# New piece orders for all engines of a two-layer transformer kernel, and one added wait

## What is computed

```python
x = x + L0_attn(layernorm(x))   # 16 heads of 16, window 64, plus a memory branch
#   q, k = rope(rms_norm(q)), rope(rms_norm(k))
#   attn_out = softmax(masked q k^T) v @ w_o
#   q_mem = (softmax(masked q k^T) * decay * gamma) k
#   phi = silu(q_mem @ mem_w1); mem_out = (phi + phi**2) @ mem_w2
#   x1 = x + attn_out * sigmoid(mem_out)
#   x1 + (silu(y @ ffn_w1) * (y @ ffn_w3)) @ ffn_w2,  y = rms_norm(x1)
x = x + L0_ffn(layernorm(x))    # relu(x @ up) @ down + sum(softmax(top2)) * (x @ expert)
x = x + L1_attn(layernorm(x))   # latent attention, 16 heads of 128, no mask
x = x + L1_ffn(layernorm(x))    # 16 experts of 176, top 6 of a softmax, plus a shared expert of 352
```

## Time and profile before

| | |
|---|---|
| median of 3 runs | 762.76 us (762.37 to 765.84) |
| the profiled execution | 762.4 us, of which the span is 760.6 and 1.8 lies around it |
| mean granted TensorE clock | 0.946 of full speed |
| PE busy | 682.0 us, 90% of the span |
| DVE, ACT, POOL busy | 416.0 us (55%), 329.3 us (43%), 259.6 us (34%) |
| transfers | 37.31 MB, mean 49 GB/s |
| the chain that ended last | PE 75%, DVE 11%, ACT 6%, issue 3%, POOL 3%, DMA 1% |

### The profile page before, as it was taken

How to read it: one execution, slowest core, us unless ns; L and a number is a source line. 1 busy time by engine, 2 the same in 40 slices (tenths; PEclk the granted TensorE clock), 3 DMA queues, 4 the chain that set the end, 5 groups by cost and what they waited for, 6 DMA issues and landing times.

```text
span 760.6 us, 13176 instructions
## 1 busy us (share of the span) xinstructions
PE 682.0 (90%) x5188; PEld 555.2 (73%) x5188; DVE 416.0 (55%) x870; ACT 329.3 (43%) x780; POOL 259.6 (34%) x340
## 2 busy tenths in 40 slices
PE   2779999999887899868699988898999999999997
PEld 1555767677776788847576867676788888888886
DVE  6566585752538665545565554545454455545455
ACT  2231644525422443345576775656443222232322
POOL 4312341521425822313535333233333333333400
PEclk9987998989999799979799999899999999999999
DMA  5322100100112200001000000000034433343201
GB/s 191 113 70 67 56 3 2 28 4 1 51 42 62 63 1 22 1 22 43 21 2 22 1 1 3 1 1 1 12 109 124 128 103 98 99 130 112 66 32 55
DMA packets 18636, 37.31 MB, mean 49 GB/s; under 512 B 2544, under 2 KB 4720, under 8 KB 18576
## 3 DMA queue, kind: packets, MB, share of 16 engines
q1 hardware_dynamic: 18576, 36.48, 15.7%
HBM read 35.19 MB, written 1.11 MB: 48 GB/s over the span
## 4 chain that ended last, share of the span: by engine, by line
PE 75%; DVE 11%; ACT 6%; issue 3%; POOL 3%; DMA 1%; DVEq 0%; SPq 0%; POOLq 0%; ACTq 0%
PE ps L615 49%; PE ps L940 4%; PE ps L758 3%; PE ps L928 3%; PE ps L734 3%; PE ps L918 2%; PE ps L693 2%; ACT AO L1217 2%; PE ps L623 2%; PE ps L637 1%; PE ps L632 1%; PE ps L641 1%; PE ps L676 1%; PE ps L708 1%; DVE sml L1621 1%
## 5 line engine op out<-in xcount | busy, mean ns | idle before, releaser
L1824 POOL TENSOR_SCALAR PB<-PB,sml 128x256 f32<-128x256 f32 x128 | 58.8, 478 | 96.7 <-DVE sml L1638 96.7
L1134 ACT CAST VVh<-U 128x512 fp32r<-128x512 f32 x50 | 31.0, 621 | 113.9 <-DVE U L1495 106.4
L615 PE MATMUL ps<-ATh,wh 128*128 128x512 f32 x176 | 71.8, 408 | 4.9 <-POOL wl L1795 3.5
L615 PE MATMUL ps<-ATh,wl 128*128 128x512 f32 x176 | 70.7, 402 | 0.0
L615 PE MATMUL ps<-ATl,wh 128*128 128x512 f32 x176 | 70.4, 400 | 0.0
L1487 DVE TENSOR_TENSOR U<-U,ps 128x512 f32<-128x512 f32 x50 | 34.4, 688 | 63.7 <-PE ps L615 61.3
L1793 POOL TENSOR_SCALAR wh<-wr 128x768 fp32r<-128x768 f32 (+3 forms) x31 | 24.6, 794 | 123.6 <-PE ps L615 122.4
L1205 ACT ACTIVATE PB<-ps,sml 128x256 f32<-128x256 f32 x128 | 59.4, 492 | 4.2 <-DVE sml L1632 4.1
L1499 DVE TENSOR_TENSOR VVl<-U,VVh 128x512 fp32r<-128x512 f32 x50 | 37.5, 750 | 37.2 <-ACT VVh L1134 37.2
L1795 POOL TENSOR_TENSOR wl<-wr,wh 128x768 fp32r<-128x768 f32 (+3 forms) x31 | 56.3, 1817 | 2.6
L1217 ACT COPY AO<-ps 128x512 f32<-128x512 f32 x64 | 35.1, 589 | 45.7 <-PE ps L928 45.5
(11 more groups left out here) (292 smaller groups left out, 2019.0 us busy)
## 6 DMA issues: line engine op xcount, KB each, us to landing
wr<-in_w SPq DMA_DIRECT2D x32, 384.0 KB, 3.1
wr<-in_w SPq DMA_DIRECT2D x16, 321.0 KB, 2.9
CB<-weights_of_experts SPq DMA_DIRECT2D x16, 256.0 KB, 3.9
wr<-in_w SPq DMA_DIRECT2D x11, 256.0 KB, 2.6
CB<-weights_of_experts SPq DMA_DIRECT2D x8, 224.0 KB, 3.6
CB<-weights_of_experts SPq DMA_DIRECT2D x8, 192.0 KB, 3.5
CB<-weights_of_experts SPq DMA_DIRECT2D x8, 160.0 KB, 3.3
XO<-in_x SPq DMA_DIRECT2D x2, 512.0 KB, 4.7
```

The lines of the kernel that those rows point to most:

```text
L615: t = x.matmul(o, a, b, start=first and i == 0 and c == 0, stop=last and i == n - 1 and c == 2, skip_group_check=skip)
L1134: x.copy((VV if run == "moe" else HH)[c][0][:, :], b[:, :]).then_inc(*mark("hi", "h", run, j, half))
L1824: t = x.tensor_scalar(p[:, c, :], p[:, c, :], m[:, 16 + c:17 + c], 1.0, ALU.mult, ALU.mult)
```

## The change

Five lists give new orders; nothing is computed differently. PROLOGUE, PERIOD and LAST are written anew. The steady loop's body becomes a list L1UNIT, and a new list END holds the pieces from the end of the attention through the first five steps of the mixture; `item()` now compares names without their "@" suffix, so that what END names isn't repeated. The wait in ACT's `step` names the right key for the ffn pieces.

What each engine's order becomes, where it differs:
- Steady iteration I. PE: turn(I-3), score(I), fill, out(I-6), weigh(I-4), where weigh stood ahead of out. ACT: hi(I-5), turn(I-3), fill, exp(I-1), where it was turn, hi, exp, fill. DVE: exp(I-1), norm(I-2), add(I-7), fill, lo(I-5), where lo stood ahead of add and fill.
- END. PE: `l1tail` ahead of weigh 29, weigh 29 and 30 ahead of turn 31, out 28 to 30 after them; down moe 0 0 behind step 2 0. ACT: turn 30 ahead of hi 28, step moe 1 0 ahead of endnorm 1. DVE: norm 31 ahead of lo 28, step moe 4 0 ahead of route 1.
- LAST, the attention and memory branch. PE: expo 3 3 ahead of step mem 0 0; step mem 0 1 and oproj 7 ahead of down mem 4 0; down mem 5 0 behind step mem 1 1, down mem 1 1 behind step mem 3 1, down mem 4 1 ahead of step mem 7 1. ACT: some oprojs earlier, step mem 1 1 ahead of oproj 7, memadd 2 ahead of step mem 4 1. DVE: weighed 3 1 ahead of step mem 1 0, memadd 2 ahead of step mem 4 1.
- LAST, the ffn. PE: down ffn 1 0 behind step ffn 4 0; down ffn 3 1 behind expert 0, step ffn 5 1 and ffndown 0. POOL: split ffn5 ahead of memturn 0; ffnmean 0 ahead of memturn 1 (its four additions into XO, L1803); latstd 0 ahead of split proj. DVE: ffnadd 1 ahead of latturn 0.
- LAST, the first units. PE: latq 0 2 ahead of l1score 1, l1weigh 1 ahead of latq 1 1. ACT: l1hi 1 ahead of latq 1 1. DVE: l1norm 2 ahead of latq 0 3. POOL: split moe1 ahead of latstd 1.
- PERIOD. PE the same. ACT: the project piece later and headnorm and parted earlier. DVE: score ahead of rope and project, POOL: rope 2 1 behind parted -1 1.
- PROLOGUE. PE: project 0 behind fuse 2, fuse 15 ahead of turnmx 0. DVE: rope 0 ahead of fuse 3, fuse 5 ahead of finish. ACT: turnqk 1 behind fuse 9 and 10. POOL: rope 3 ahead of finish 2.

The diff, cut to its core:

```diff
 LAST = [
...
-    "down ffn 2 1", "up@p 0", "up@a 0", "up@v 0", "step@p ffn 4 1", "l1begin@p",
-    "step@a ffn 4 1", "step@v ffn 4 1", "expert@a 0", "down ffn 3 1", "step@a ffn 5 1", "expert@p 0", "expert@v 0",
-    "step@p ffn 5 1", "step@v ffn 5 1", "ffndown@p 0", "ffndown@v 0", "latstd@v 0", "down ffn 4 1", "split proj",
-    "down ffn 5 1", "latturn@v 0", "ffnadd 1", "latnorm 0", "latturn@p 0", "l1begin@v", "ffnmean@v 1", "latstd@g 0",
...
+    "step@v ffn 4 1", "expert@a 0", "expert@v 0", "step@a ffn 5 1", "expert@g 0", "latstd@g 0", "expert@p 0",
+    "step@p ffn 5 1", "step@v ffn 5 1", "ffndown@p 0", "ffndown@v 0", "latstd@v 0", "ffnadd 1", "down ffn 3 1",
+    "down ffn 4 1", "down ffn 5 1", "split proj", "latnorm 0", "latturn@v 0", "l1begin@v", "ffnmean@v 1", "latturn@a 0",
...
+L1UNIT = [
+    "l1hi 5", "l1norm@g 2", "l1turn@p 3", "l1turn@a 3", "l1exp@v 1", "l1norm@v 2", "l1score 0", "add 7", "l1lo 5",
+    "fill 0", "l1out 6", "l1exp@a 1", "l1weigh 4",
+]
+END = [
+    "l1turn@p 30", "l1turn@a 30", "l1norm@g 31", "l1out 27", "l1hi 28", "l1tail", "l1norm@v 31", "l1hi 29", "l1weigh 29",
+    "l1weigh 30", "endnorm@g 1", "l1lo 28", "l1turn@p 31", "l1turn@a 31", "l1out 28", "l1lo 29", "l1lo 30", "l1lo 31",
+    "l1add 3", "l1weigh 31", "l1hi 30", "split moe3", "split moe4", "endnorm@v 1", "step@v moe 0 0", "step@v moe 1 0",
...
+]
@@ plan() @@
     def item(*a):
-        if a not in ahead:
+        if (a[0].partition("@")[0], *a[1:]) not in ahead:
             order.append(a)
...
-        if unit(3):
-            item("l1turn", i - 3)
-        if unit(5):
-            item("l1hi", i - 5)
-        if unit(1):
-            item("l1exp", i - 1)
-        if unit(2):
-            item("l1norm", i - 2)
-        if unit(5):
-            item("l1lo", i - 5)
-        if unit(7) and us[i - 7][1] == 7:
-            item("l1add", us[i - 7][0])
-        if unit(0):
-            item("l1score", i)
-            for f in fill.get(us[i], ()):
-                freed(f) if isinstance(f, str) else item(*f)
-        if unit(4):
-            item("l1weigh", i - 4)
-        if unit(6):
-            item("l1out", i - 6)
...
+        for text in L1UNIT:
+            kind, d = text.split()
+            u = i - int(d)
+            if not 0 <= u < n:
+                continue
+            if kind == "fill":
+                for f in fill.get(us[u], ()):
+                    freed(f) if isinstance(f, str) else item(*f)
+            elif kind != "add":
+                item(kind, u)
+            elif us[u][1] == 7:
+                item("l1add", us[u][0])
+    for text in END:
+        kind, *a = text.split()
+        a = [int(v) if v.isdigit() else v for v in a]
+        order.append((kind, *a))
+        ahead.add((kind.partition("@")[0], *a))
+    state["next"] = SPLIT.index("moe7")
+    state["open"] = 9
@@ scalar(), step() @@
             if i >= 3:
-                e.wait_ge(*at("hh", "moe" if i - 3 >= 28 else "mem", i - 3))
+                e.wait_ge(*at("hh", "moe" if i >= 31 else "ffn" if i >= 19 else "mem", i - 3))
```

More of the change, by code:

```diff
@@ L145 @@
 PROLOGUE = [
[15 rows of a table removed]
[15 rows of a table added]
 ]
 PERIOD = [
[9 rows of a table removed]
[9 rows of a table added]
 ]
 LAST = [
[27 rows of a table removed]
-    "step@a ffn 2 1", "split exp", "ffnturn@v 0", "step@p ffn 3 1", "ffnturn@a 0", "step@v ffn 3 1", "step@a ffn 3 1",
-    "split down", "expert@g 0", "down ffn 2 1", "up@p 0", "up@a 0", "up@v 0", "step@p ffn 4 1", "l1begin@p",
-    "step@a ffn 4 1", "step@v ffn 4 1", "expert@a 0", "down ffn 3 1", "step@a ffn 5 1", "expert@p 0", "expert@v 0",
-    "step@p ffn 5 1", "step@v ffn 5 1", "ffndown@p 0", "ffndown@v 0", "latstd@v 0", "down ffn 4 1", "split proj",
[14 rows of a table removed]
[6 rows of a table added]
+    "mlpwide", "step@a mem 2 0", "split mem4", "oproj@p 5", "oproj@a 4", "step@a mem 3 0", "step@p mem 3 0",
[20 rows of a table added]
+    "step@v ffn 2 1", "split exp", "split down", "ffnturn@v 0", "step@p ffn 3 1", "ffnturn@a 0", "step@a ffn 3 1",
[3 rows of a table added]
+    "down ffn 4 1", "down ffn 5 1", "split proj", "latnorm 0", "latturn@v 0", "l1begin@v", "ffnmean@v 1", "latturn@a 0",
[13 rows of a table added]
+]
[4 more added lines that the diff above has]
+END = [
[10 rows of a table added]
 ]
@@ L332, in plan @@
     for i in range(n + 1):
-        def unit(d):
-            return 0 <= i - d < n
         if i == 3:
             item("l1rings")
-        if unit(3):
-            item("l1turn", i - 3)
-        if unit(5):
-            item("l1hi", i - 5)
-        if unit(1):
-            item("l1exp", i - 1)
-        if unit(2):
-            item("l1norm", i - 2)
-        if unit(5):
-            item("l1lo", i - 5)
-        if unit(7) and us[i - 7][1] == 7:
-            item("l1add", us[i - 7][0])
-        if unit(0):
-            item("l1score", i)
-            for f in fill.get(us[i], ()):
-                freed(f) if isinstance(f, str) else item(*f)
-        if unit(4):
-            item("l1weigh", i - 4)
-        if unit(6):
-            item("l1out", i - 6)
-    item("l1tail")
-    for kind, d in (("hi", 4), ("lo", 4), ("norm", 1), ("turn", 2), ("weigh", 3), ("out", 5), ("hi", 3), ("lo", 3),
-                    ("weigh", 2), ("out", 4), ("turn", 1), ("hi", 2), ("lo", 2), ("out", 3), ("weigh", 1), ("out", 2),
-                    ("hi", 1), ("lo", 1), ("out", 1)):
-        item("l1" + kind, n - d)
-    item("l1add", 3)
-    item("moebegin")
-    item("endnorm@v", 1)
-    item("endnorm@g", 1)
-    split(9)
+        for text in L1UNIT:
[17 more added lines that the diff above has]
+    state["open"] = 9
     def moe_after(half):
```

## The result

Four executions of the changed kernel gave a median of 740.17 us (737.88 to 743.82) beside 762.57 for the kernel before; the ratio is 0.970, interval 0.965 to 0.976. Two later sets of 4 and 6 executions had medians of 748.3 and 744.4, ratios 0.979 (0.971 to 0.987) and 0.976 (0.970 to 0.983). The ratios leave out executions that were over 1.5% above the fastest of their kernel and set; medians and means here keep all. Over all fourteen the median is 744.0 and the mean 744.8. The profiled execution took 737.88 us (span 736.0); its lines carry numbers two higher than those of before, so L942 is the weighing, L617 the three-part product, L1230 the layernorm on ACT.

A forecast was written before the change was run, and what follows sets the result against it. TensorE (PE), busy 90% of the span, was taken as the bound, so only its waits and half-clocked stretches could be won. The terms summed to -12.1 us, from 762.4 to 750.3, as median 750.7; range 744.5 to 758.

The forecast's parts named there:

- NB: Layernorm stall at 321 us, PE waiting 5.1 us: expert work starts earlier and the split moves behind the rsqrt; -2.5 us.
- The steady units: Second attention's unit loop: ACT's copies leave the loop, so the weighing's 7.2 us wait for the low part shrinks; -6.7 us.
- wl: Mem6 stall in layer 0, PE waiting 2.5 us for a split: matmuls of down mem 4 0 fill it; -1.4 us.
- HHl: Rms stall at 241.9 us, 6.6 us: the third addition on DVE runs before POOL's split; -1.0 us.
- XO: First scores, 3.2 us wait: a query piece fills PE, while POOL's moved split delays the layernorm; -0.4 us.
- +0.7: POOL's four moved additions, beside DVE's ffn steps: one DVE loss of up to 1.54 us, half behind PE work.
- Unit 22: Layernorm stall in the second attention, 5.1 us: DVE's addition now stands ahead of the low part; -0.5 us.
- The mixture: PE busy 199.27 of 200 us, nothing to win; a change above one us would show the forecast wrong.
- Prologue, periods, END: The three other reordered lists: 0 us each, bounds -1 to +1, for the periods -1 to +2.
- The added wait: ACT's ffn hidden copy waits for PE's down product three pieces earlier, already covered by DVE's product; 0 us.
- Rival 3: Filled units: exponentials behind the fill come late and the weighing waits again, 16 us, giving 767; chance 0.04.
- Rival 1: Layer 0's gains reappear at the next waits and only the steady term stays, 756.1 us; chance 0.24.

The follow-up runs named there:

- e8: Changed kernel with ACT's part of the last layernorm's first half one unit later and DVE's low part back ahead of addition and fill; median 742.6 us.
- e9: Kernel before with one exchange in the steady iteration: ACT takes the high part ahead of the copies; ratio 0.987, 9.5 us less at equal clock.
- e2: Kernel before with the new LAST alone and the added wait; median 756.0 us, ratio 0.990.
- e14: Kernel before with ACT's high part first and its exponentials behind the fill, PE's and DVE's order as before; 751.1 us at equal clock.
- e10: Kernel before with PE's output product ahead of the weighing alone, ACT still copying first; ratio 0.996, 4.6 us less at equal clock.
- e3: Kernel before with the new steady iteration alone and the added wait; ratio 0.991, 7.0 us less at equal clock.
- e7: Changed kernel with the old order from the end of the second attention on; four executions, 739.4 to 752.1 us.
- e4: Kernel before with the new END alone and the added wait; median 761.7 us, ratio 0.998.

## Why the prediction was right or wrong

**The step that failed is the sum's silence on the clock.** Every stall was priced by the time that PE stands still in it, and the clock was put at nothing; it stands in the bounds of one stall alone. At equal clock the forecast of -12.1 stands against -13.1, or -11.9 to -13.5 by the slopes of the two families. The rest of the difference is the granted clock: over fourteen executions it is worth 5.7 us, over the first four 8.4 (0.957 against 0.943), of which some 4 us were luck. The part that stays is bound to the places that I had looked at: from the first hidden piece to the last weighing the kernel before spends 42 us at half clock, the changed one 32.9 and 34.1 in its profiles of 737.9 and 739.9 us. At the stall for NB that is 10.2 against 6.8, from the first exponentials of the second attention to its first weighing 10.2 (in other profiles with the old LAST also 6.8) against 3.4 and 6.8, and from there to the last weighing 10.2 against 6.8. A stall's worth has to be counted with the half-clock stretch near it, and rows 2 had it in plain view (0.66 from 245 to 260 us). The other part, ahead of the first hidden piece, comes and goes with the execution in both kernels, and no order here controls it: two executions of the changed kernel spent 28 and 66 us at half clock there, and took 737.9 and 762.6 us. What makes the clock fall is open: some stretches follow a stall, and others, as in e8, don't.

**The steady units: right.** -6.7 was forecast; the new iteration alone measures -7.0 at equal clock, and L940's waits went from 7.2 us to none. The reading of the loop in rows 4 holds: ACT's copies stood ahead of the high part. A unit takes 3.85 us, 0.11 above the 3.74 that I took for PE's own work. What I described as one edit are two, and each alone ends the wait; e9, with ACT's alone, gains more (9.5 us) than the whole iteration does, and why is open.

**The waits of LAST: right in the sum, by luck in part.** -0.3 -1.4 -1.0 -2.5 -0.4 +0.7 = -4.9 was forecast, and e2 measures -4.9 at equal clock (6.3 by the medians, with its clock as it came). Term by term the lists of waits differ from it: wl -1.4 as forecast; NB -2.6 where I had -2.5; HHl -2.1 where I had -1.0; xl +0.5 where I had -0.3; XO, for which I had -0.4, nothing. Two links are as I read them: the rsqrt L1303 takes 0.17 us, and DVE's L1512, 1.97 us before, now takes 0.93 for the third addition, but step 4 1 and the fourth addition's first half meet the split instead (0.69 and 0.41 us where POOL isn't working):

```profile
229.96 0.93 DVE L1512 SCALAR_TENSOR_TENSOR X<-T,X 128x256 f32<-128x256 f32 x1
230.82 2.33 DVE L1484 SCALAR_TENSOR_TENSOR T<-T 128x512 f32<-128x512 f32 x1
...
234.44 2.08 DVE L1509 SCALAR_TENSOR_TENSOR T<-T,AO 128x256 f32<-128x256 f32 x1
```

The four additions that moved to 286 us (3.29 us) cost no wait of PE that the lists show, so the +0.7 was too much. The changed kernel's trace says why:

```profile
286.37 3.29 POOL L1805 TENSOR_TENSOR XO<-XO,X 128x256 f32<-128x256 f32 x4
```

```profile
287.60 0.76 DVE L1501 TENSOR_TENSOR HHl<-T,HHh 128x512 fp32r<-128x512 f32 x1 [0.74 <-ACT HHh L1136]
```

In these 3.29 us DVE ran one whole instruction whose two inputs both lie outside PSUM, the low part, in 0.76 us where it takes 0.69 alone. The third addition, which began beside it, took 1.20 us, and the others 0.73 to 0.75. So DVE lost 0.07 us and POOL 0.46. The Trainium skill (SBUF — State Buffer, "SBUF: two separate sides") has the pair of ports go to whichever starts first, for the whole instruction. The trace agrees in kind, since DVE had started first; but what I worked out from that rule, a DVE instruction blocked by every addition, +3.3, needed a DVE instruction beside each of the four, and there was one.

**Unit 22: the number right, the reason not shown.** -0.5 forecast, 5.1 to 4.5. I had put it down to DVE's addition, which now stands ahead of the low part. But e9 leaves DVE's order as it was and has 4.1 us there, e14 as well, and e10, without ACT's exchange, 5.2. What shortens this stall comes with the high part first on ACT.

**The mixture: it moved by more than I allowed.** PE waits 1.7 us there in one piece, where it was 2.6 in three, and the stage from its first Silu to its last is 208.3 us, where it was 210.0. I had named a change of more than 1 us here as a sign of a wrong forecast. But e2 and e3, which have the order of the kernel before in the mixture, took 209.0, so 1 of the 1.7 us is not the order's; the other 0.7 is END's, as e7 (209.0) and e4 (208.3) show.

**Prologue, periods, END: 0 each was too coarse.** At equal clock -2.2, +0.8 and -1.7. The first and the last lie outside the bounds of 1 us that I gave. For END I said that its three banks for the last weighings were counted in the steady term; they weren't: e4's list of waits still has the 7.2 us in 11 pieces, and from the first to the last weighing e4 wins 1.1 us all the same, as the changed kernel does over e7. The -2.2 of PROLOGUE and the +0.8 of PERIOD weren't traced to a wait of their size.

**The added wait: no cost seen.** ACT's list of waits from 230 to 312 us has its copies behind DVE's products alone, none behind PE. The first copy that the new wait holds, which is the one of rows 7, waits 3.97 us for DVE's product, and PE waits for nothing from 255 to 312 us:

```profile
ACT HHh L1136 <- DVE T L1489: 19.3, 12, 4.0
ACT HHh L1136 <- DVE T L1484: 12.7, 4, 5.6
```

**Three readings that were wrong.** PE's 682.0 us are 1.6 times DVE's 416.0, not twice. The prologue has not one wait of 6.1 us but also one of 8.2 (NB) and one of 5.6 (the first transfer), which the new order left as they were. And the range's lower end of 744.5 doesn't follow from the two bounds named for it, which make 747.2 (1.5 us for NB, 2 for the rms stall). None of the three changes the sum.

**The rivals.** None came about. Rival 3 had its mechanism examined by e3 and e14: 0.5 us in one wait. The margin held. Rival 1 (gains of layer 0 given back) is refuted by e2.

## What to carry to other kernels

Where one engine evacuates two results in a loop, have it serve first the one that frees the scarcer buffer; here that one exchange on ACT was worth 9.5 us of 762 (four executions, at equal clock), and 7.0 as part of the whole new iteration. When a profile is compared with another, compare the granted clock of the same stretch first, and bring the times of many executions to one clock: it tells parts of 2 us apart where medians scatter by 5. Then ask separately what the order did to the clock, which a time at equal clock hides. Here fewer and shorter stalls in the ffn and at the start of the second attention came with some 10 us less at half clock; but when one stall of 4.5 us went, its 6.8 us at half clock were still there in three profiles of four, in other places.

## What the runs showed of the hardware that I had not expected

With one program on one core the granted clock varied between executions: in the changed kernel from 0.930 to 0.959, and the time from 738 to 763 us, in steps rather than evenly. Its fourteen clocks take the values 0.958 or 0.959 (six times), 0.954 (four), and 0.950, 0.947, 0.945 or 0.930. About half of the time at half clock lies ahead of 200 us (31 of 63 us in the profile of 737.9 us). A busy PE, by the profile's measure, was no guard against the lower clock: in e8 it fell at 488 us, when PE had been busy for 18.00 of 18.00 us, and from 65 to 80 us of the kernel before it was low while PE was busy for 13.84 of 15. Transposes in a stall weren't one either.
